# Which engine turns the softmax weights, pair by pair, and how turned blocks travel, in a two-layer attention kernel

## Chip, cores and metric

One core of a Trainium2 chip. The metric is the device time of one execution in microseconds.

## The reference

Sixteen batch entries of 256 tokens x 256 channels go through two layers. Layer 0 is attention of x on ctx_1024 with 16 heads of 64 channels, an output product, a residual and a layer norm. Layer 1 is masked self attention (16 heads of 16), cross attention on ctx_1024 (16 heads of 16), and an MLP of width 1024, each with residual and layer norm. Cut to what matters, one attention is

```python
scores = jnp.einsum('bqhd,bkhd->bhqk', qh, kh) / jnp.sqrt(jnp.float32(hd))
scores = jnp.where(mask != 0, jnp.finfo(scores.dtype).min, scores)
p = jax.nn.softmax(scores, axis=-1)
out = jnp.einsum('bhqk,bkhd->bqhd', p, vh)
```

All three attentions are over 256 keys. They are called A (layer 0), B (self) and C (cross).

## The kernel before

Scores are computed with queries on the partitions, so that the softmax sums run along the free dimension. The weighing of the values contracts over the keys, so every 256 x 256 matrix of softmax weights must be turned, keys onto the partitions.

**Pairs, quads, places.** Heads go two at a time as pairs (e = 0 and 1) and four at a time as quads; an attention has 8 pairs, 4 quads. The kernel is software pipelined over batch entries: a body works on five of them at once (streams x, a, b, c, m). Twelve bodies are full (n = 4 to 15); four fill the pipeline and a last one, written out by hand in `last_schedule`, empties it. A full body has 24 places, one for each pair, in the quad order AAABCBACBBCC: A0 to A5 are places 0 to 5, B0 B1 are 6 and 7, C0 C1 8 and 9, B2 B3 10 and 11, A6 A7 12 and 13, C2 C3 14 and 15, B4 to B7 16 to 19, C4 to C7 20 to 23.

**The list of steps.** `Line.advance` writes one list of steps, and each engine walks through it in this order and does the steps that are its own, with semaphores between the engines. An engine's queue is in order. A place g holds:
- S: TensorE computes the scores of the pair into two of three PSUM banks (ps_s0, ps_s1, ps_av in rotation); VectorE (`extremes`, L1071) masks them and takes the extreme of each row, in four instructions, into the prob tile. TensorE may begin the next place's S when the first head of this one is masked.
- R: VectorE takes the reciprocals of the previous place's pair (L1081), for which ScalarE's sums must be there; then POOL (`normalize`, L1182) scales this pair's two heads by them and counts up `normed`. POOL's residual steps (L1173, L1161, L1170) come after.
- D: VectorE's `turn_blocks` (L1093) turns 32 x 32 blocks of the pair two places back into the tile `blocks`; SyncE's `spill` (L595) writes it with four DMAs to DRAM. L: `load_back` (L602), a place later, reads it into `prob_b`, keys on the partitions.
- T0, T1: TensorE turns one head each of the pair three places back (L797) into ps_t0 and ps_t1. VectorE (L1102) copies a first pair of a quad out, ScalarE (L911) a second pair.
- jobs: the projections, output products and MLP parts set down for this place (`after` in `schedule`), with their evacuations on VectorE or ScalarE.
- W: TensorE weighs the values with the quad whose second pair is four places back (L820), in full bodies into ps_t1. X: ScalarE's exponentials of this place's pair (L901). AV: the weighed values are copied out, by ScalarE or, for every other quad of B and C, VectorE (L1114).

In full bodies the first pair of each quad, whichever attention, is turned by VectorE in blocks through DRAM, at even places only, and the second by TensorE, with tile `prob_t`. In the other bodies TensorE turns both. The order at a place is S, R, D, L, T0, jobs, W, T1, X, AV. SyncE's queue issues all transfers, in the order of the list.

Of the kernel before, what the change touches and what calls it, by code (L numbers as in the profile page):

```python
# [11 lines left out]
F32 = mybir.dt.float32  # L12
# [5 lines left out]
P = 128  # L18
# [22 lines left out]
BLOCKED = {(s, q) for s in "ABC" for q in range(QUADS)}  # L41
# [23 lines left out]
class Line:  # L65
# [4 lines left out]
    def __init__(self, steps, carried, blocked):  # L70
        self.steps = steps
        self.pairs = {g - len(carried): (p[1:], b) for g, (p, b) in enumerate(carried)}
        self.blocked = blocked
        self.places = 0

    def score(self, *pair):
        self.pairs[self.places] = pair, (pair[0], pair[1] // 2) in self.blocked
        self.steps.append(("S",) + pair)

    def advance(self, jobs):  # L80


        g, pairs, steps = self.places, self.pairs, self.steps

        def older(back, parity, by_blocks=None):
            pair, blocked = pairs.get(g - back, (None, None))
            return pair if pair and pair[1] % 2 == parity and by_blocks in (None, blocked) else None
# [11 lines left out]
        weigh = older(LAG + 1, 1)  # L99
        quad = weigh and (weigh[0], weigh[1] // 2, weigh[2])  # L100
        if quad:
            steps.append(("W",) + quad)
        if turn:
            steps.append(("T1",) + turn)
# [235 lines left out]
def program(nc, io):  # L340
    with ExitStack() as ctx:
# [27 lines left out]
        x_t, c_t = sb("x_t", [P, DT, TOK]), sb("c_t", [P, DT, TOK])  # L369
# [6 lines left out]
        prob_t = sb("prob_t", [P, 2, TT, TOK])  # L376


        blocks = sb("blocks", [P, 4, TT * 2 * TT * SLOT])
        prob_b = sb("prob_b", [P, 2, 4, TT * 2 * TT * SLOT])  # L380
# [8 lines left out]
        v_next = sb("v_next", [P, TT, D])  # L389
# [22 lines left out]
        x_cols_in, c_cols_in = sem("x_cols_in"), sem("c_cols_in")  # L412
# [18 lines left out]
        spilled = sem("spilled")  # L431
        landed = [sem("landed0"), sem("landed1")]
        p_kept = [nc.dram_tensor(f"p_kept{i}", (P, 4, TT * 2 * TT * SLOT), F32) for i in range(2)]
# [24 lines left out]
        x_cols, c_cols = (tok_view(io[n]) for n in ("x_cols", "ctx_cols"))  # L458
# [46 lines left out]
        def _(sp):  # L505
# [9 lines left out]
            def load_columns(body, step):  # L515
# [8 lines left out]
                sp.dma_start(c_t[:, :, :].unsqueeze(1), c_cols[:, bass.ds(b, 1)]).then_inc(c_cols_in, 16)  # L524

# [60 lines left out]
            def spill(body, step):  # L586

                _, s, p, _ = step
                n = body.turned_so(body.quad(step), True)
                sp.wait_ge(flipped, n + 1)  # L590
                if n >= 2:
                    sp.wait_ge(landed[n % 2], 16 * (n // 2))
                by_key = p_kept[n % 2].rearrange("(g r) q x -> q r g x", r=SLOT)
                for q in range(4):
                    sp.dma_start(by_key[q], blocks[q * SLOT:(q + 1) * SLOT, :, :]).then_inc(spilled, 16)  # L595

            def load_back(body, step):
                n = body.turned_so(body.quad(step), True)
                sp.wait_ge(spilled, 64 * (n + 1))
                (_, s0, p0, _), b0 = body.pair_at(body.place(step) - 4)  # L600
                sp.wait_ge(weighed[s0], count(b0, QUADS, p0 // 2 + 1))
                sp.dma_start(prob_b[:, body.quad(step) % 2], p_kept[n % 2][:, :, :]).then_inc(landed[n % 2], 16)  # L602
# [22 lines left out]
            for body in bodies():  # L625
                for step in body.steps:
                    if step[0] == "D":
                        spill(body, step)
                    elif step[0] == "L":
                        load_back(body, step)  # L630
# [13 lines left out]
        def _(pe):  # L644
# [49 lines left out]
            def job(body, step):  # L694
# [8 lines left out]
                if name in ("q", "k"):  # L703
# [3 lines left out]
                    last = columns_out(ps, wq0 if name == "q" else wk0, 2 * i, x_t if name == "q" else c_t)  # L707
# [5 lines left out]
                elif name == "kc":  # L713
                    if first:
                        pe.wait_ge(w_in["attn1"], 16)
                    last = columns_out(ps, w1["ck"], 0, c_t)
# [61 lines left out]
            def turn(body, step, e):  # L778
# [4 lines left out]
                quad = body.quad(step)  # L783
                if p % 2 and not body.by_blocks[quad]:
                    pe.wait_ge(copied_first, 2 * body.turned_so(quad, False) + e + 1)
                elif quad:
                    pe.wait_ge(copied_second, 2 * (quad - 1) + e + 1)
# [13 lines left out]
            def weigh(body, step):  # L801
# [4 lines left out]
                firsts = body.turned_so(n, by_blocks)  # L806
                if by_blocks:
                    pe.wait_ge(landed[firsts % 2], 16 * (firsts // 2 + 1))
                else:
                    pe.wait_ge(copied_first, 2 * (firsts + 1))  # L810
                pe.wait_ge(copied_second, 2 * (n + 1))
                by_query = prob_b[:, n % 2].rearrange("p q (k e t r) -> p k e t q r", k=TT, e=2, t=TT)
                by_head = prob_b[:, n % 2].rearrange("p q x -> p (q x)").rearrange("p (e k n) -> p e k n", e=2, k=TT)

                def weighted(out, w, j, e, kt, **tile):
                    by_block = j == 0 and by_blocks
                    turned_pair = by_query[:, kt, e] if by_block else (prob_t[:, e, kt] if j else by_head[:, e, kt])
                    if by_block:
                        out = out.rearrange("p (t q r) -> p t q r", t=TT, r=SLOT)
# [415 lines left out]
```

## Time and profile before

| what | value |
|---|---|
| median of 3 runs | 1815.4 us (1813.83 to 1820.91) |
| profiled execution, its time | 1820.59 us |
| its span, first to last instruction | 1818.4 us |
| TensorE matmul busy | 1714.5 us (94%), 11328 instructions |
| VectorE busy | 1270.7 us (70%), 4778 |
| ScalarE busy | 1190.7 us (65%), 3985 |
| POOL busy | 985.4 us (54%), 1014 |
| mean granted TensorE clock | 0.988 |
| SyncE's DMA queue | 321.73 MB, 56.3% of the 16 engines' span |

Times are microseconds from the first instruction unless marked ns. Busy means that an instruction is under way; a matmul's end is modelled and matmuls overlap, so what one costs is read from start to start. In a list of groups, "idle" is the time in which the engine stood still just before them, behind the arrow what ended it.

### The profile page before, as it was taken

How to read it: one execution, taken by the hardware profiler on the slowest of the kernel's cores; microseconds unless marked ns; L12 is line 12 of the kernel's file. 1: busy time of each engine (PE TensorE's matmuls, PEld its weight loads, DVE VectorE, ACT ScalarE, POOL GpSimd, SP SyncE). 2: the span in 40 equal slices, each digit the busy share in tenths (PEclk: the TensorE clock that was granted, in tenths of full speed). 3: DMA queues.
4: the chain of work that ended last, by engine and by line, in shares of the span. 5: the costliest groups of instructions: out<-in, count | busy, mean ns of one | idle time of the engine just before them, and what ended most of it. 6: DMA issues, size and time to landing. Idle time of an engine off the chain costs nothing.

```text
span 1818.4 us, 36921 instructions
## 1 busy us (share of the span) xinstructions
PE 1714.5 (94%) x11328; PEld 1284.8 (71%) x11328; DVE 1270.7 (70%) x4778; ACT 1190.7 (65%) x3985; POOL 985.4 (54%) x1014
## 2 busy tenths in 40 slices
PE   8999999999999999999999999999999999998887
PEld 6777677777777777677777767777777777776556
DVE  4465766786768778676877858687786867667763
ACT  4374866667676666767666666776667677566752
POOL 2252745547465564747556464655647465455742
PEclk9999999999999999999999999999999999998899
DMA  7222226685766768576676847668575766613010
GB/s 252 89 97 100 82 79 216 181 279 158 238 192 203 251 172 277 163 249 185 204 250 175 280 134 240 207 192 264 179 253 158 242 214 175 198 65 134 30 58 12
DMA packets 215696, 324.11 MB, mean 178 GB/s; under 512 B 22992, under 2 KB 184144, under 8 KB 207056
## 3 DMA queue, kind: packets, MB, share of 16 engines
q1 hardware_dynamic: 215360, 321.73, 56.3%
q8 instruction: 95, 1.56, 0.4%
q14 instruction: 97, 0.79, 0.1%
q10 hardware_dynamic: 144, 0.03, 0.0%
HBM read 170.68 MB, written 150.99 MB: 177 GB/s over the span
## 4 chain that ended last, share of the span: by engine, by line
PE 77%; DMA 7%; DVE 6%; ACT 5%; SPq 3%; issue 2%; POOL 0%; POOLq 0%; DVEq 0%; ACTq 0%
PE ps_g L654 45%; PE ps_t L797 10%; PE ps_s L773 8%; PE ps_t L820 8%; DMA prob_b<-p_kept 4%; ACT prob L901 3%; DMA p_kept<-blocks 3%; PE ps_av L773 3%; PE ps_av L820 3%; DVE prob L1071 2%; SPq L595 1%; SPq L578 1%; PE ps_g L660 1%; DVE prob_b L1102 1%; DVE blocks L1093 1%
## 5 line engine op out<-in xcount | busy, mean ns | idle before, releaser
L1182 POOL TENSOR_TENSOR prob<-prob,recip 128x512 f32<-128x512 f32 x768 | 788.2, 1048 | 668.4 <-DVE recip L1081 668.1
L901 ACT ACTIVATE prob<-prob,ext 128x256 f32<-128x256 f32 x1536 | 757.2, 499 | 11.9 <-DVE ext L1071 11.5
L911 ACT ACTIVATE prob_t<-ps_t 128x512 f32<-128x512 f32 x384 | 226.4, 594 | 397.2 <-PE ps_t L797 396.5
L797 PE MATMUL ps_t<-ident,prob 128*128 128x128 f32 x1920 | 304.1, 283 | 7.2 <-DVE prob_b L1102 5.4
L901 ACT ACTIVATION_READ_ACCUMULATOR prob<-prob,ext 128x1 f32 x1536 | 295.6, 192 | 0.0
L797 PEld LDWEIGHTS ps_t<-ident,prob 128*128 128x128 f32 x1920 | 216.7, 142 | 93.3 <-issue 49.7
L1071 DVE CUSTOM_DVE_ANT_0 prob<-ps_s,mask_a 128x256 f32<-128x256 f32 x392 | 145.4, 421 | 84.0 <-PE ps_s L773 70.6
L1093 DVE STREAM_TRANSPOSE blocks<-prob 128x512 f32<-128x512 f32 x288 | 183.9, 676 | 3.1 <-POOL prob L1182 2.2
L1071 DVE CUSTOM_DVE_ANT_0 prob<-ps_s,zero 128x256 f32<-128x256 f32 x392 | 144.4, 418 | 47.0 <-PE ps_av L773 39.6
L1071 DVE CUSTOM_DVE_ANT_0 prob<-ps_s,mask_b 128x256 f32<-128x256 f32 x368 | 136.0, 417 | 24.3 <-PE ps_s L773 14.7
L773 PE MATMUL ps_s<-k_ctx,q 64*128 64x256 f32 x784 | 144.8, 402 | 5.5 <-DVE ext L1071 3.1
L654 PE MATMUL ps_g<-wo,k_ctx 128*128 128x256 f32 x512 | 121.0, 392 | 22.6 <-ACT k_ctx L920 21.6
L654 PE MATMUL ps_g<-x_t,wq 128*128 128x256 f32 x512 | 124.3, 386 | 5.8 <-DMA wq<-L_xattn_Wq 5.8
L1071 DVE DVE_READ_ACCUMULATOR2_ANT ext<- 128x1 f32 x1536 | 126.7, 82 | 0.0
L654 PEld LDWEIGHTS ps_g<-wo,k_ctx 128*128 128x128 f32 x512 | 97.2, 194 | 40.5 <-issue 26.1
L654 PE MATMUL ps_g<-c_t,wk 128*128 128x256 f32 x512 | 125.6, 388 | 0.0
L654 PE MATMUL ps_g<-x_t,wl 128*128 128x256 f32 x512 | 123.1, 384 | 1.2 <-ACT x_t L880 1.2
L654 PE MATMUL ps_g<-wv,c_t 128*128 128x256 f32 x512 | 121.0, 379 | 0.0
L654 PE MATMUL ps_g<-wl,h_t 128*128 128x256 f32 x512 | 116.8, 383 | 2.0 <-issue 2.0
L773 PEld LDWEIGHTS ps_s<-k_ctx,q 64*128 64x128 f32 x784 | 87.5, 186 | 32.6 <-issue 28.9
L654 PEld LDWEIGHTS ps_g<-x_t,wq 128*128 128x128 f32 x512 | 94.9, 192 | 19.4 <-issue 6.4
L654 PEld LDWEIGHTS ps_g<-wl,h_t 128*128 128x128 f32 x512 | 96.2, 192 | 14.9 <-issue 2.7
(104 smaller groups left out, 2967.7 us busy)
## 6 DMA issues: line engine op xcount, KB each, us to landing
p_kept<-blocks SPq DMA_DIRECT2D x576, 128.0 KB, 2.5
prob_b<-p_kept SPq DMA_DIRECT2D x144, 512.0 KB, 3.4
k_parts_C<-k_hl SPq DMA_DIRECT2D x64, 256.0 KB, 3.1
k_parts_B<-k_hl SPq DMA_DIRECT2D x64, 256.0 KB, 3.0
q_parts_B<-q_hl SPq DMA_DIRECT2D x64, 256.0 KB, 3.4
k_B<-k_parts_B SPq DMA_DIRECT2D x16, 1024.0 KB, 7.4
q_B<-q_parts_B SPq DMA_DIRECT2D x16, 1024.0 KB, 7.2
q_parts_C<-k_hl SPq DMA_DIRECT2D x64, 256.0 KB, 4.9
```

Of the source, the lines that this page charges most:

```text
L578: sp.dma_start(q_parts[s][:, part].rearrange("e r c t -> (r c) e t"), parts[:, part // 2]).then_inc(q_saved[s], 16)
L595: sp.dma_start(by_key[q], blocks[q * SLOT:(q + 1) * SLOT, :, :]).then_inc(spilled, 16)
L654: last = nc.tensor.matmul(out, lhs[i], rhs[i], start=i == 0, stop=i == n - 1)
L660: last = nc.tensor.transpose(ps[:, d, t * P:(t + 1) * P], src[:, t, d * P:(d + 1) * P], ident[:, :])
L773: last = nc.tensor.matmul(two(score_bank(body, step, e))[:, t, :], q[r, t * P:(t + 1) * P], k[r], start=True, stop=True)
L797: last = nc.tensor.transpose(two(ps_t[e])[:, kt, qt * P:(qt + 1) * P], src[:, e, qt, kt * P:(kt + 1) * P], ident[:, :])
L820: return nc.tensor.matmul(out, w, turned_pair, start=kt == 0, stop=kt == TT - 1, **tile)
L901: last = nc.scalar.activation(tile, tile, ACT.Exp, bias=ext[:, slot, e, t:t + 1], scale=-1.0, accum_out=sums[:, slot, e, t:t + 1])
L911: nc.scalar.activation(prob_t[:, e], two(ps_t[e]), ACT.Copy).then_inc(copied_second, 1)
L1071: last = nc.vector.tensor_tensor_reduce(out=prob[:, slot, e, t, :], in0=two(score_bank(body, step, e))[:, t, :], in1=mask, scale=-SCALE[s] ...
L1093: last = nc.vector.transpose(out[:, kt], src[:, kt])
L1182: nc.gpsimd.tensor_tensor(rows, rows, recip[:, slot, e].unsqueeze(2) .to_broadcast([P, TT, TOK]), ALU.mult).then_inc(normed[s], 1)
```

## The change

Which pairs are turned how. In full bodies all pairs of A and C (16 of 24) are now turned by VectorE in blocks, all pairs of B (8) by TensorE. The first pair of a B quad is copied out of PSUM by VectorE, the second by ScalarE; both now land in `prob_b`, and `prob_t` is gone.

How the blocks travel. `blocks` and `prob_b` hold both pairs of a quad and are double. `turn_blocks` is one instruction over 1024 columns instead of two over 512. DRAM is not used any more: after the second pair of a quad is turned, SyncE's `exchange` issues four DMAs of 256 KB straight from the partitions of `blocks` to those of `prob_b`, when the quad two before has been weighed. That needs another order of the keys: a new input `ctx_keys` holds the context in that order, and the masks of A are permuted likewise; a tile `c_k` takes its columns for the key projections. It shares its memory with `v_next`, so that its load waits for `v_saved`.

Order in a place. D stands first, in front of S (`begin` is called by `score`). Where TensorE turns a first pair at a place that also has a W, T1 follows T0 directly, ahead of jobs and W, and W waits for VectorE's copies of both. The order is D, S, R, T0, (T1), jobs, W, (T1), X, AV.

```diff
-BLOCKED = {(s, q) for s in "ABC" for q in range(QUADS)}
+BLOCKED_BATCHES = {"A": range(3, 15), "C": range(1, 13)}
+BLOCKED = {(s, q) for s in "AC" for q in range(QUADS)}
...
+    def begin(self):
+
+        if self.begun == self.places:
+            self.begun += 1
+            if self.older(BLOCKS, None, True):
+                self.steps.append(("D",) + self.older(BLOCKS, None, True))
 
     def score(self, *pair):
+        self.begin()
         self.pairs[self.places] = pair, (pair[0], pair[1] // 2) in self.blocked
         self.steps.append(("S",) + pair)
 
     def advance(self, jobs):
...
+        self.begin()
         if g - 1 in pairs:
             steps.append(("R",) + pairs[g - 1][0])
-        if older(BLOCKS, 0, True):
-            steps.append(("D",) + older(BLOCKS, 0, True))
-        if older(BLOCKS + 1, 0, True):
-            steps.append(("L",) + older(BLOCKS + 1, 0, True))
-        turn = older(LAG, 0, False) or older(LAG, 1)
+        turn = older(LAG, None, False)
+        weigh = older(LAG + 1, 1)
+        quad = weigh and (weigh[0], weigh[1] // 2, weigh[2])
+        early = turn and turn[1] % 2 == 0 and quad and self.blocked
         if turn:
             steps.append(("T0",) + turn)
+        if early:
+            steps.append(("T1",) + turn)
         steps.extend(jobs)
...
         if quad:
             steps.append(("W",) + quad)
-        if turn:
+        if turn and not early:
             steps.append(("T1",) + turn)
...
@@ load_columns
                 sp.dma_start(c_t[:, :, :].unsqueeze(1), c_cols[:, bass.ds(b, 1)]).then_inc(c_cols_in, 16)
+                sp.wait_ge(v_saved, count(b - 1, 16, 16))
+                sp.dma_start(c_k[:, :, :].unsqueeze(1), c_keys[:, bass.ds(b, 1)]).then_inc(c_keys_in, 16)
...
@@ spill and load_back, now exchange
+            def exchange(body, step):
+
+                quad = body.quad(step)
+                n = body.turned_so(quad, True)
+                sp.wait_ge(flipped, 2 * n + 2)
+                (_, s0, p0, _), b0 = body.pair_at(2 * quad - 4)
+                sp.wait_ge(weighed[s0], count(b0, QUADS, p0 // 2 + 1))
                 for q in range(4):
...
+                    sp.dma_start(prob_b[:, quad % 2, q].rearrange("p j x -> p (j x)"),
+                                 blocks[q * SLOT:(q + 1) * SLOT, n % 2].rearrange("r g j x -> r g (j x)")
+                                 ).then_inc(landed[n % 2], 16)
...
             sp.dma_start(c_t[:, :, :], c_cols[:, 0]).then_inc(c_cols_in, 16)
+            sp.dma_start(c_k[:, :, :], c_keys[:, 0]).then_inc(c_keys_in, 16)
...
@@ weigh
+                if by_blocks:
+                    k = body.turned_so(n, True)
+                    pe.wait_ge(landed[k % 2], 64 * (k // 2 + 1))
+                pe.wait_ge(copied_second, 2 * body.turned_so(n + 1, False))
+                if body.full:
+                    pe.wait_ge(copied_first, 2 * body.turned_so(n + 2, False))
...
@@ turn_blocks
+                n = body.turned_so(body.quad(step), True)
                 dve.wait_ge(normed[s], count(body.batch(step), HEADS, 2 * p + 2))
...
-                for kt in range(TT):
-                    last = nc.vector.transpose(out[:, kt], src[:, kt])
-                last.then_inc(flipped, 1)
+                if n >= 2 and p % 2 == 0:
+                    dve.wait_ge(landed[n % 2], 64 * (n // 2))
+                src = prob[:, body.slot(step, P_RING)].rearrange("p e t (k g r) -> p (e t k) g r", k=TT, r=SLOT)
+                out = blocks[:, n % 2, :, p % 2].rearrange("p g (m q) -> p m g q", q=SLOT)
+                nc.vector.transpose(out, src).then_inc(flipped, 1)
```

## Rows read from the trace of the kernel before

**Rows 1.** Page, the chain that ended last: shares of the span.
```profile
PE 77%; DMA 7%; DVE 6%; ACT 5%; SPq 3%; issue 2%; POOL 0%; POOLq 0%; DVEq 0%; ACTq 0%
```

**Rows 2.** Waits: engine line <- what it waited for: us, times, longest.
```profile
DVE prob L1071 <- PE ps_s L773: 178.5, 144, 4.5
...
DVE prob L1071 <- PE ps_av L773: 62.4, 48, 6.2
...
PE ps_s L773 <- DVE ext L1071: 20.0, 23, 2.3
...
DVE blocks L1093 <- POOL prob L1182: 2.2, 12, 0.2
```

**Rows 3.** Windows: us, busy (x instructions) by engine, clock, DMA share, GB/s.
```profile
445.00:1500.00 1055.00, 1018.87 (x6769) 764.18 (x6771) 781.99 (x2945) 731.90 (x2459) 609.06 (x622) 1.00 0.69 214
...
1660.00:1680.00 20.00, 14.65 (x105) 10.07 (x105) 16.17 (x60) 14.42 (x49) 9.98 (x11) 0.83 0.45 158
```

**Rows 4.** Timeline of SyncE: start, us; two issues one body apart.
```profile
902.46 0.38 SPq L571 DMA_DIRECT2D k_C<-k_parts_C  x1
...
1008.37 0.38 SPq L571 DMA_DIRECT2D k_C<-k_parts_C  x1
```

**Rows 5.** Timeline, PE at place 0: half a turn, then a projection.
```profile
902.46 0.66 PE L797 MATMUL ps_t<-ident,prob 128*128 128x128 f32 x4
...
902.95 1.89 PE L654 MATMUL ps_g<-w_l,ctx_B 128*128 128x256 f32 x8
```

**Rows 6.** Timeline, DVE at places 0 and 1: start, duration.
```profile
902.69 0.42 DVE L1071 CUSTOM_DVE_ANT_0 prob<-ps_s,mask_a 128x256 f32<-128x256 f32 x1 [0.79 <-PE ps_s L773]
...
904.17 1.27 DVE L1093 STREAM_TRANSPOSE blocks<-prob 128x512 f32<-128x512 f32 x2
...
905.37 0.65 DVE L1029 TENSOR_TENSOR res_ln<-ps_g,res_ln 128x512 f32<-128x512 f32 x1
...
908.56 0.41 DVE L1071 CUSTOM_DVE_ANT_0 prob<-ps_av,mask_a 128x256 f32<-128x256 f32 x1
...
912.62 0.68 DVE L986 COPY v<-ps_g 128x512 f32<-128x512 f32 x1
```

**Rows 7.** Groups by form, VectorE's copies: xcount | busy, mean ns | idle.
```profile
L1102 DVE COPY prob_b<-ps_t 128x512 f32<-128x512 f32 x96 | 64.4, 675 | 44.7 <-PE ps_t L797 44.2
```

**Rows 8.** Timeline: DVE and POOL where a turn waits for POOL.
```profile
966.84 0.18 DVE L1081 RECIPROCAL recip<-sums 128x4 f32<-128x4 f32 x1
...
967.10 3.04 POOL L1182 TENSOR_TENSOR prob<-prob,recip 128x512 f32<-128x512 f32 x3 [0.89 <-DVE recip L1081]
...
969.17 1.30 DVE L1093 STREAM_TRANSPOSE blocks<-prob 128x512 f32<-128x512 f32 x2 [0.18 <-POOL prob L1182]
```

**Rows 9.** Timeline, DVE: first extremes of places 7, 11, 14, 17, 21.
```profile
937.63 0.42 DVE L1071 CUSTOM_DVE_ANT_0 prob<-ps_av,mask_b 128x256 f32<-128x256 f32 x1 [0.28 <-PE ps_s L773]
...
955.17 0.39 DVE L1071 CUSTOM_DVE_ANT_0 prob<-ps_s,mask_b 128x256 f32<-128x256 f32 x1
...
966.96 0.42 DVE L1071 CUSTOM_DVE_ANT_0 prob<-ps_s,zero 128x256 f32<-128x256 f32 x1
...
980.17 0.42 DVE L1071 CUSTOM_DVE_ANT_0 prob<-ps_s,mask_b 128x256 f32<-128x256 f32 x1 [0.84 <-PE ps_av L773]
...
998.09 0.39 DVE L1071 CUSTOM_DVE_ANT_0 prob<-ps_s,zero 128x256 f32<-128x256 f32 x1
```

**Rows 10.** Timeline, DVE at place 21: reciprocal.
```profile
1000.37 0.18 DVE L1081 RECIPROCAL recip<-sums 128x4 f32<-128x4 f32 x1 [0.85 <-ACT prob L901]
```

**Rows 11.** Timeline, POOL at place 7: first residual step.
```profile
941.93 1.28 POOL L1173 TENSOR_TENSOR res_ln<-res_ln,rows 128x512 f32<-128x512 f32 x1
```

**Rows 12.** Timeline, PE at place 18: output product.
```profile
985.06 1.10 PE L654 MATMUL ps_g<-wo,k_ctx 128*128 128x256 f32 x4 [1.72 <-ACT k_ctx L920]
```

**Rows 13.** DMA issues: xcount, KB each, median us to landing.
```profile
p_kept<-blocks SPq DMA_DIRECT2D x576, 128.0 KB, 2.5
...
q_B<-q_parts_B SPq DMA_DIRECT2D x16, 1024.0 KB, 7.2
```

More of the change, by code:

```diff
@@ L73, in __init__, with older @@
         self.blocked = blocked
-        self.places = 0
+        self.places = self.begun = 0
+    def older(self, back, parity=None, by_blocks=None):
+        pair, blocked = self.pairs.get(self.places - back, (None, None))
+        return pair if pair and parity in (None, pair[1] % 2) and by_blocks in (None, blocked) else None
+    def begin(self):
[3 more added lines that the diff above has]
+                self.steps.append(("D",) + self.older(BLOCKS, None, True))
     def score(self, *pair):
+        self.begin()
         self.pairs[self.places] = pair, (pair[0], pair[1] // 2) in self.blocked
@@ L457, in program @@
         x_d, m_d, o_d = (tok_view(io[n]) for n in ("x", "mask_BxSxS2_bf0", "out"))
-        x_cols, c_cols = (tok_view(io[n]) for n in ("x_cols", "ctx_cols"))
+        x_cols, c_cols, c_keys = (tok_view(io[n]) for n in ("x_cols", "ctx_cols", "ctx_keys"))
         wide = lambda n: io[n].rearrange("(k p) n -> p k n", p=P)
@@ L626, in _ @@
                 for step in body.steps:
[L627 to L630, printed above, removed]
+                    if step[0] == "D" and step[2] % 2:
+                        exchange(body, step)
                     elif step[0] == "IO":
@@ L715, in job @@
                         pe.wait_ge(w_in["attn1"], 16)
-                    last = columns_out(ps, w1["ck"], 0, c_t)
+                    pe.wait_ge(c_keys_in, count(b, 16, 16))
+                    last = columns_out(ps, w1["ck"], 0, c_k if b in BLOCKED_BATCHES["C"] else c_t)
                 elif name == "vc":
@@ L781, in turn @@
                 pe.wait_ge(normed[s], count(body.batch(step), HEADS, 2 * p + e + 1))
[L783 to L787, printed above, removed]
+                n = body.turned_so(body.quad(step), False)
+                if p % 2:
+                    pe.wait_ge(copied_first, 2 * n + e + 1)
+                elif n:
+                    pe.wait_ge(copied_second, 2 * (n - 1) + e + 1)
                 if e == 1:
@@ L909, in evac_turned @@
                 quad = body.quad(step)
-                act.wait_ge(turned, 2 * (quad + body.turned_so(quad + 1, False)) + e + 1)
-                nc.scalar.activation(prob_t[:, e], two(ps_t[e]), ACT.Copy).then_inc(copied_second, 1)
+                act.wait_ge(turned, 2 * (2 * body.turned_so(quad, False) + 1) + e + 1)
+                out = prob_b[:, quad % 2].rearrange("p q j x -> p (q j x)")[:, (2 + e) * 512:(3 + e) * 512]
+                nc.scalar.activation(out, ps_t[e][:, :], ACT.Copy).then_inc(copied_second, 1)
             def evac_weighed(body, step):
@@ L1100, in evac_turned @@
                 quad = body.quad(step)
-                dve.wait_ge(turned, 2 * (quad + body.turned_so(quad, False)) + e + 1)
-                nc.vector.tensor_copy(prob_b[:, quad % 2].rearrange("p q x -> p (q x)")[:, e * 512:(e + 1) * 512],
-                                      ps_t[e][:, :]).then_inc(copied_first, 1)
+                dve.wait_ge(turned, 2 * 2 * body.turned_so(quad, False) + e + 1)
+                out = prob_b[:, quad % 2].rearrange("p q j x -> p (q j x)")[:, e * 512:(e + 1) * 512]
+                nc.vector.tensor_copy(out, ps_t[e][:, :]).then_inc(copied_first, 1)
             def evac_weighed(body, step):
@@ L1215, in laid_out @@
     arrays["x_cols"] = np.swapaxes(given["x"], 1, 2)
+    by_block = lambda a: np.swapaxes(a.reshape(*a.shape[:-1], TT, SLOT, P // SLOT), -1, -2).reshape(a.shape)
+    arrays["ctx_keys"] = by_block(np.swapaxes(given["ctx_1024"], 1, 2))
+    mask = given["mask_BxSxS2_bf0"].copy()
+    for b in BLOCKED_BATCHES["A"]:
+        mask[b] = by_block(mask[b])
+    arrays["mask_BxSxS2_bf0"] = mask
     arrays["ctx_cols"] = np.swapaxes(given["ctx_1024"], 1, 2)
```

64 lines of the change are left out of this document (19 added, 45 removed).

## The prediction

> **What bounds the kernel now.** I read the chain of waits first: TensorE holds 77% of it, DMA 7%, VectorE 6% [rows 1]. Then the list of waits: VectorE waits for a score product 178.5 and 62.4 us in all (two banks), TensorE for VectorE's extremes 20.0 us, and a turn of VectorE's for POOL 2.2 us [rows 2]. So TensorE sets the pace, VectorE runs just behind it with short rests. Third, the windows: from 445 to 1500 us TensorE is busy 1018.87 of 1055, 97%, VectorE 74%, at a granted clock of 1.00 [rows 3]. One full body takes 1008.37 - 902.46 = 105.9 us, between two issues of the same DMA [rows 4]; it has 24 places, 4.4 us each, and there are 12 full bodies. I number places 0 (A0) to 23 (C7) and write S7 for the start of VectorE's extremes of place 7.
>
> **What the change takes from TensorE.** Before, TensorE turns 12 pairs of a body, after only B's 8. Half a pair holds the engine from 902.46 to 902.95, 0.49 us [rows 5], a pair about 1.0. Four pairs are 4 us of a body, 48 us in all (2.7%), if TensorE remains the limit. ScalarE loses 16 copies of a body; it lies beside TensorE and I count nothing. The weighing keeps its number of products.
>
> **What it gives VectorE.** Before: 12 turns at 1.20 us (904.17 to 905.37 [rows 6]), 14.4. After: 16 at the same price (one instruction of 1024 columns for two of 512), 19.2; bounds for one turn are the two instructions' 1.27 on top and 1.1 below, if a start is saved. Each B quad's first pair also needs two copies from PSUM of 675 ns [rows 7], eight in a body, 5.4. VectorE gets 10 us more: 74% of 105.9 is 78.5, so 88.7 of a body. As a mean that still fits.
>
> **Where it does not fit: the order of the turn.** Before, VectorE took at a place: the extremes, the reciprocal of the previous pair, then the turn of the pair two back, then jobs. The turn came after the extremes, and at even places only. Now the turn stands in front of the extremes, at 16 of 24 places. It waits until POOL has scaled both heads of the pair two back, and POOL starts that when VectorE has done the pair's reciprocal, which stands behind the previous place's extremes. Behind the waiting turn stand this place's extremes, on which ScalarE's exponentials and TensorE's next scores depend. This closes a ring over four steps:
> extremes to the next instruction after the reciprocal 904.17 - 902.69 = 1.48 [rows 6], of which the reciprocal's step is 0.09; reciprocal to the end of POOL's scaling, seen where a turn does wait for POOL: 966.84 to 969.17, 2.33 [rows 8]; turn 1.20. So 1.39 + 2.33 + 1.20 = 4.92 us from S to S wherever a turn stands in front, however short TensorE's work there is. Jobs of the place run inside the 2.33; where they are longer, they replace it.
>
> Hence one body, in five stretches, after against before (the starts in [rows 9], the body's end 105.91 later):
> - S21 to S7, ten intervals, each with a turn in front: 10 x 4.92 = 49.2. Jobs of place 0 run 905.37 to 908.56, 3.19, and those of place 1 from 910.04 (S1 at 908.56 plus 1.48) to some 913.24, 3.2 [rows 6]; each makes 1.48 + 3.2 + 1.2 = 5.9, so 1.0 more, twice. The reciprocal of place 20's pair waited 0.85 for ScalarE [rows 10] and still will. 52.0. Before 1043.54 - 998.09 = 45.5.
> - S7 to S11: POOL is late first. From S7: 1.65 to its start, then scaling 2.04, the two residual steps of place 7 at 1.28 and a gap, 2.6 [rows 8, 11], two more scalings, turn 1.24: 11.6 to S10; then 4.9. 16.5. Before 17.5.
> - S11 to S14: 1.65, three scalings 6.1, three residual steps 3.9 (1.3 each), turn 1.24: 12.9. Before 11.8.
> - S14 to S17: three rings, 14.8. Before 13.2.
> - S17 to S21: one turn fewer in front, and TensorE's work is as before (one pair less at 18, one more at 19): 17.9 before, with a wait of 1.72 of the output product for ScalarE [rows 12] that is shorter by perhaps 0.4. 17.5.
>
> Sum 113.7, before 105.9: 7.8 a body, 93 us in twelve. Inside it lies one more new wait: at place 13 the weighing of C0 has no job ahead of it and must wait for VectorE's two copies, as ps_t1 holds both; TensorE's scores and turn end 2.1 us after place 13's start, the copies 1.3 + 1.5 + 1.3 = 4.1 after it, 2 us. There VectorE, not TensorE, sets the next S, so it is not added. The TensorE saving is hidden by the ring wherever S is late.
>
> **DMA.** Spill and load go (12 x 1 MB moved in a body), 8 exchanges of 1 MB come, each from the second pair's turn on, four issues. Nearest rows: four spills are 128 KB each, 2.5 us to landing; the 1 MB load of spread queries 7.2 us [rows 13]. With 1.8 us of issue the exchange takes between 4.3 and 9.0 us. Time to have it hidden: shortest at place 17 (A3): turn done at S15, S15 to S17 is 9.8; TensorE may start place 17 when half the extremes of 16 are done, 0.8 after S16, so 4.1 before S17, and the weighing follows 0.4 behind the scores: 6.1 us. At others over 7. I take 6 us, nothing; at 9.0, 2.9 at place 17 and up to 2 more at places 5 and 3, of which half reaches S: 3 us a body, 35 us. The Trainium skill (DMA: Bandwidth & Descriptors, Anatomy of one DMA) fits a DMA from the other issue path with 2.0 us plus bytes over 436 GB/s; by that 1 MB is an estimated 4.4 us, nothing would be late, and the sum stays 113.7. No run so far shows an exchange between partitions. The new loads of ctx_keys wait for the saved values at place 17, one DMA; exchanges behind it come at place 23. At the start 256 KB stand ahead of the weights: 1 us.
>
> **Sum.** The profiled execution took 1820.6 us (span 1818.4), the median of the runs is 1815.4. 1820.6 + 93 + 1 = 1914.6; less the same 5.2 that the profiled one stands above the median: 1909.
>
> **Rivals.**
> 1. *TensorE stays the limit.* VectorE waits for TensorE anyway, 178.5 us in all, and the ring runs in that shadow. For it: the turn in front uses just this rest. Against: the rest is (178.5 + 62.4) / 16 = 15 us a batch, 0.6 a place, while TensorE's places of the first stretch would shrink to (45.5 - 4 pairs + 1) / 10, 4.3 us, against a ring of 4.92. It decides if the ring is under some 4.3 us, POOL's part under 1.7. Then -48, +24 for place 13 (2 us x 12): 1791.
> 2. *The gain and the ring cancel.* If VectorE catches up at the places with much TensorE work better than I count, half of each stretch's excess is lost: at most 0.5% from before, 1815.
> 3. *The exchange is late, the ring is not the bound.* At 9 us it misses by 2.5 at place 17, 1.4 at 7 and about 1.5 at 3, where it stands behind the query saves on SP's queue: 5.4 a body, 65 on top of rival 1: 1856.
> 4. *The clock falls too.* TensorE's work of a body, 102.3 less 4, is 86% of 113.7. At 1660 to 1680, where it was busy 73%, the granted clock was 0.83, part of the time the lower of the two levels, 1.2 GHz [rows 3]. On the ring TensorE's speed costs nothing; on the last stretch, S7 to S9 and place 11, some 30 us a body, a clock of 0.9 costs up to 3: 36 us more, 1945. For it that row; against it that no wait in the ring is over 2.5 us.
>
> **How the numbers follow.** The ring alone 0.62; with a fallen clock or late exchange 0.22; rival 3 alone 0.03; rival 2 0.04; rival 1 0.09. A measurement here tells about 0.5% from no change. Slower: 0.87, same 0.04, faster 0.09. The predicted time is 1909. The range reaches down to 1850, where the ring costs 3 us a body instead of 7.8 (turns at 1.1, and TensorE ahead more often), and up to 1955 for a fallen clock; this leaves out rivals 1 and 2 and little above.
>
> **What would show it.** The body is 113 to 114 us; VectorE's blocks<-prob waits for POOL's scaling at most of 16 places, some 170 us in all, up to 2.2 us each at places without jobs, where before it waited 2.2 us in all; TensorE's scores wait for the extremes, far over 20 us; TensorE's share in the windows falls from 97% to about 90%, its turns are 1536 products in place of 1920. S to S is 4.9 from place 2 to place 7. The forecast is wrong if the turns are found waiting for nothing, with TensorE still at 96%; if the scores hold the turn's place open; or if the weighing waits for prob_b<-blocks in place of VectorE.

## The result: slower by 11.7%, and what the profile shows

The changed kernel takes 2032.1 us, the median of four runs (2012.0 to 2041.1), against 1815.5 of the kernel before: ratio 1.117 [1.108, 1.126]. Forecast were 1909 and a range up to 1955, so the sign was right and the size was 123 us short. The profiled execution took 2041.1 us, with a span of 2039.3. The rows of this section are read from it.

From the page: busy times, shares of the chain that ended last, the DMA groups of the exchange and of the spread queries (KB each, median us to landing).
```profile
PE 1778.2 (87%) x10944; PEld 1295.8 (64%) x10944; DVE 1385.0 (68%) x4778; ACT 1113.6 (55%) x3793; POOL 984.8 (48%) x1014
...
PE 55%; DVE 15%; issue 8%; SPq 7%; DMA 7%; POOL 4%; ACT 3%; DVEq 0%; POOLq 0%
...
prob_b<-blocks SPq DMA_DIRECT2D x384, 256.0 KB, 4.8
q_B<-q_parts_B SPq DMA_DIRECT2D x16, 1024.0 KB, 9.3
```
TensorE held 77% of the chain before [rows 1] and holds 55% now. VectorE, POOL, SyncE's queue and the engine's own issue have taken the rest. TensorE is busy 87% of the span, no other engine more than 68%, so most of the loss must lie in waits of one engine for another; a second part, TensorE's lower clock, comes up in the windows.

The list of waits: us in all, times, longest.
```profile
ACT prob L907 <- DVE ext L1078: 289.0, 158, 4.4
DVE prob L1078 <- PE ps_s L778: 168.4, 120, 6.5
...
PEld ps_t L826 <- DMA prob_b<-blocks: 117.8, 40, 6.1
PE ps_t L826 <- DMA prob_b<-blocks: 104.2, 39, 5.7
...
DVE blocks L1099 <- POOL prob L1187: 100.9, 96, 2.2
...
DVE prob L1078 <- PE ps_av L778: 68.1, 13, 8.3
...
PE ps_s L778 <- DVE ext L1078: 33.1, 43, 2.4
```
Two waits are new. VectorE's turn waits for POOL's scaling 100.9 us, against 2.2 [rows 2], and never over 2.2 us at once. The weighing waits for the exchange 104.2 us, up to 5.7 us at once; no such wait stands in [rows 2]. The prediction named this second wait as a sign that it is wrong. (The `PEld` row is the weight load for the same products, not a second cost.)

The windows of the steady part, the columns of [rows 3].
```profile
445.00:1500.00 1055.00, 913.69 (x5558) 659.77 (x5558) 749.69 (x2527) 576.58 (x1988) 525.69 (x538) 0.93 0.53 148
```
TensorE is busy 87% of it (before 97%), at a granted clock of 0.93 (before 1.00).

SyncE's timeline, the issue that gave the body's length in [rows 4], first and last of eleven bodies.
```profile
390.69 0.55 SPq L576 DMA_DIRECT2D k_C<-k_parts_C  x1
...
1759.36 0.55 SPq L576 DMA_DIRECT2D k_C<-k_parts_C  x1
```
1368.67 / 11 = 124.4 us a body. Before it was 106.6 by the same mean (105.9 in the body that the prediction used); forecast 113.7. The 17.8 us a body, twelve times, are 214 of the 217 us lost.

VectorE's timeline of one body, the first extremes of places 7, 11, 14, 17 and 21, which answer to [rows 9].
```profile
1056.42 0.39 DVE L1078 CUSTOM_DVE_ANT_0 prob<-ps_av,mask_b 128x256 f32<-128x256 f32 x1
...
1075.96 0.39 DVE L1078 CUSTOM_DVE_ANT_0 prob<-ps_s,mask_b 128x256 f32<-128x256 f32 x1
...
1088.66 0.39 DVE L1078 CUSTOM_DVE_ANT_0 prob<-ps_s,zero 128x256 f32<-128x256 f32 x1
...
1104.26 0.39 DVE L1078 CUSTOM_DVE_ANT_0 prob<-ps_s,mask_b 128x256 f32<-128x256 f32 x1
...
1123.04 0.42 DVE L1078 CUSTOM_DVE_ANT_0 prob<-ps_s,zero 128x256 f32<-128x256 f32 x1 [1.07 <-PE ps_s L778]
```
With the same starts of the experiments below, one body of each, this gives the five stretches of the prediction (the first ends at S7 and begins at S21 of the body before):

| us | S21 to S7 | S7 to S11 | S11 to S14 | S14 to S17 | S17 to S21 | sum |
|---|---|---|---|---|---|---|
| before (prediction's body) | 45.5 | 17.5 | 11.8 | 13.2 | 17.9 | 105.9 |
| forecast | 52.0 | 16.5 | 12.9 | 14.8 | 17.5 | 113.7 |
| after | 56.1 | 19.5 | 12.7 | 15.6 | 18.8 | 122.7 |
| no exchange | 54.2 | 16.3 | 12.7 | 17.1 | 18.8 | 119.0 |
| turn after extremes | 51.0 | 21.5 | 14.1 | 13.3 | 23.0 | 122.9 |
| neither | 49.4 | 15.9 | 14.1 | 15.0 | 17.2 | 111.7 |
| neither, copies by ScalarE | 47.0 | 15.9 | 12.9 | 13.3 | 17.2 | 106.4 |

A single body can stand off the mean: over the full bodies "neither" has a mean of 110.0 us, the others 119.5 (no exchange), 122.3 (turn after extremes) and 107.2 (the last row).

### The profile page after: what moved, and what is told of

It is laid out like the page before. It is cut to its first block, busy times and chain, and to the rows that moved or that the text cites. A ratio compares the mean times of both kernels' runs of the same rounds, so it can differ in the third digit from the quotient of the medians.

```text
span 2039.3 us, 35276 instructions
## 1 busy us (share of the span) xinstructions
PE 1778.2 (87%) x10944; PEld 1295.8 (64%) x10944; DVE 1385.0 (68%) x4778; ACT 1113.6 (55%) x3793; POOL 984.8 (48%) x1014
## 4 chain that ended last, share of the span: by engine, by line
PE 55%; DVE 15%; issue 8%; SPq 7%; DMA 7%; POOL 4%; ACT 3%; DVEq 0%; POOLq 0%
PE ps_g L652 32%; PE ps_t L802 7%; PE ps_t L826 6%; DVE prob L1078 6%; PE ps_s L778 5%; SPq L599 5%; DMA prob_b<-blocks 4%; POOL prob L1187 4%; PE ps_av L826 2%; DMA q_parts_C<-k_hl 2%; SPq L583 2%; DVE res_ln L1054 2%; ACT prob L907 1%; DVE blocks L1099 1%; PE ps_av L778 1%
## 5 line engine op out<-in xcount | busy, mean ns | idle before, releaser
L1099 DVE STREAM_TRANSPOSE blocks<-prob 128x1024 f32<-128x1024 f32 x192 | 237.8, 1238 | 102.1 <-POOL prob L1187 100.9
L802 PE MATMUL ps_t<-ident,prob 128*128 128x128 f32 x1536 | 241.8, 287 | 6.2 <-DVE prob_b L1108 5.1
L918 ACT ACTIVATE prob_b<-ps_t 128x512 f32<-128x512 f32 x192 | 112.7, 596 | 218.5 <-PE ps_t L802 217.9
L826 PE MATMUL ps_t<-prob_b,v 128*64 128x256 f32 x768 | 134.1, 510 | 101.5 <-DMA prob_b<-blocks 101.5
L802 PEld LDWEIGHTS ps_t<-ident,prob 128*128 128x128 f32 x1536 | 172.0, 144 | 71.6 <-issue 36.9
L826 PEld LDWEIGHTS ps_t<-prob_b,v 128*64 128x64 f32 x768 | 67.0, 180 | 155.6 <-DMA prob_b<-blocks 113.5
L1108 DVE COPY prob_b<-ps_t 128x512 f32<-128x512 f32 x192 | 124.6, 672 | 45.7 <-PE ps_t L802 45.2
L652 PE MATMUL ps_g<-wo,k_ctx 128*128 128x256 f32 x512 | 133.3, 421 | 24.2 <-ACT k_ctx L927 23.2
L652 PE MATMUL ps_g<-x_t,wq 128*128 128x256 f32 x512 | 137.4, 417 | 7.0 <-DMA wq<-L_xattn_Wq 7.0
L894 ACT ACTIVATE k_ctx<-ps_g,columns 128x256 f32<-128x256 f32 x128 | 53.2, 466 | 119.6 <-PE ps_g L652 119.5
```

What stands on the lines that cost most here:

```text
L652: last = nc.tensor.matmul(out, lhs[i], rhs[i], start=i == 0, stop=i == n - 1)
L802: last = nc.tensor.transpose(two(ps_t[e])[:, kt, qt * P:(qt + 1) * P], src[:, e, qt, kt * P:(kt + 1) * P], ident[:, :])
L826: return nc.tensor.matmul(out, w, turned_pair, start=kt == 0, stop=kt == TT - 1, **tile)
L894: last = nc.scalar.activation(out[:, c, :], ps[:, m, :], ACT.Relu if name == "h" else ACT.Identity, bias=bias[:, c:c + 1])
L918: nc.scalar.activation(out, ps_t[e][:, :], ACT.Copy).then_inc(copied_second, 1)
L1099: nc.vector.transpose(out, src).then_inc(flipped, 1)
```

## The experiments

Theory 1: the ring of the prediction, closed by the turn's place in front of the extremes, costs most. Theory 2: the exchange arrives late. The first three runs take the two apart.

**No exchange.** The weighing reads the turned tile itself. `prob_b` plays no part for A and C, and VectorE's turn waits, in place of the landing, until the quad that held its buffer has been weighed. What this kernel leaves out is the crossing of the partitions.

```diff
-                    if step[0] == "D" and step[2] % 2:
-                        exchange(body, step)
...
-                    pe.wait_ge(landed[k % 2], 64 * (k // 2 + 1))
+                    pe.wait_ge(flipped, 2 * k + 2)
...
-                by_query = [prob_b[:, n % 2, :, j]
+                by_query = [blocks[:, k % 2, :, j]
```

> The weighing reads the blocks where VectorE left them, without any exchange (so the weighed values of A and C are left wrong in full bodies); the turn still stands in front. Theory ring (VectorE turn waits for POOL, about 4.9 us from extremes to extremes, is a bound of its own): a body of about 114 us, 1910 to 1930 us in all, the turns still waiting some 100 to 170 us for POOL. Theory exchange (the late transfer is the whole loss and the ring lies in its shadow): about 1800 us.

Measured: 1970.1 us, 1.082 [1.079, 1.085]. Waits:
```profile
DVE blocks L1100 <- POOL prob L1188: 129.7, 108, 2.2
```
Without any exchange some 150 us of loss remain (the kernel before took 1819.1 us in this round).

**The turn after the extremes.** The exchange stays; D goes back behind R.

```diff
 begin:
-            if self.older(BLOCKS, None, True):
-                self.steps.append(("D",) + self.older(BLOCKS, None, True))
 advance, behind R:
+        if older(BLOCKS, None, True):
+            steps.append(("D",) + older(BLOCKS, None, True))
```

> The changed kernel with the turn put back behind extremes and reciprocal of its place. Theory ring: the 7.8 us a body of the prediction go, 93 us, to about 1940 us, and the turns wait under 10 us for POOL. Theory exchange: the exchange starts 1.4 us later at each quad and the weighings wait that much longer, 2030 us or more.

Measured: 2013.6 us, 1.106 [1.102, 1.109]. Waits:
```profile
PE ps_t L826 <- DMA prob_b<-blocks: 143.8, 47, 5.1
```
No wait of a turn for POOL is in its list, so the ring is open, and yet only 18.5 us come back, hardly more than the spread of the runs (the two intervals touch): the wait for the exchange grew from 104 to 144 us.

**Neither**, both edits at once.

> Both: no exchange (weighed values wrong in full bodies) and the turn behind the extremes. Theory that these two are all of the loss: what is left is TensorE less four pairs a body plus the wait at place 13, 1790 to 1815 us. If a third cause exists (VectorE's 10 us more of work a body), 1830 or more.

Measured: 1857.8 us, 1.021 [1.018, 1.025]. That is 174 us under the changed kernel, where the two edits alone gave 62 and 18.5. The ring alone costs 1970.1 - 1857.8 = 112 us, the exchange alone 2013.6 - 1857.8 = 156, both together 174, not 268. The two costs overlap. If they are two bounds on the same starts, at each place only the later one counts; a run below tests that. And 1857.8 is above the 1830 that the expectation gave for a third cause.

**SyncE's queue in another order.** The save of the self queries, the load of the cross values and the load of the cross queries are issued later, behind exchanges.

```diff
-        ("A", 0): late + [dma("save k", "B"), job("ks"), dma("save q", "B")],
-        ("A", 1): [dma("k", "B"), job("qs"), ln("ln1"), job("v", 0)],
-        ("A", 2): [job("x2T"), dma("q", "B"), job("q", 2), job("qc"), io("value_c")],
+        ("A", 0): late + [dma("save k", "B"), job("ks")],
+        ("A", 1): [dma("k", "B"), job("qs"), dma("save q", "B"), ln("ln1"), job("v", 0)],
+        ("A", 2): [job("x2T"), dma("q", "B"), job("q", 2), job("qc")],
...
-        ("A", 4): [dma("q", "C"), job("oc"), job("vs")],
-        ("A", 5): [ln("ln2")],
+        ("A", 4): [job("oc"), job("vs")],
+        ("A", 5): [dma("q", "C"), io("value_c"), ln("ln2")],
```

> The changed kernel with four steps moved in SyncE's queue so that no exchange of places 1, 3 and 5 stands behind a save of queries or the load of values or of C's queries. Theory that the place in the queue makes the exchange late: the exchanges of A0 and A1 start 3.4 and 5.7 us earlier, and 5 to 7 us a body go, to 1950 to 1975 us. Theory that issue and transfer are the delay: within 1% of the changed kernel, 2015 to 2050 us.

Measured: 2024.1 us, 1.112 [1.109, 1.116], as the second theory had it and not the first. But the place in the queue does matter at each single place: place 7 became short (2.58 us instead of 5.51), place 5 as much longer (9.80 instead of 6.80). The longest wait moved from one exchange to another and the sum stayed.

**The kernel before with its turns in front.** The twelve turns of [rows 6] are put ahead of the extremes; all else is the kernel before.

```diff
     def score(self, *pair):
+        pair2, blocked2 = self.pairs.get(self.places - BLOCKS, (None, None))
+        if pair2 and pair2[1] % 2 == 0 and blocked2:
+            self.steps.append(("D",) + pair2)
...
-        if older(BLOCKS, 0, True):
-            steps.append(("D",) + older(BLOCKS, 0, True))
```

> The kernel before with one change: its turns, still at even places only, stand in front of the extremes. Theory ring, needed only where it is longer than the place: intervals into even places that are under 4.85 us fall short by 9 us a body, but every second interval has no turn in front and gives most of it back: 1 to 3 us a body, 1830 to 1855 us. If the position of the turn alone were the price, whatever the spacing, half of e1's ring cost of 9.4 us a body: 1870 us.

Measured: 1829.5 us, 1.009 [1.006, 1.012]. Waits:
```profile
DVE blocks L1094 <- POOL prob L1183: 108.3, 76, 2.2
```
The turn waits 108 us for POOL, as much as in the changed kernel, and it costs 15 us. With a turn only at even places the place between catches up. The wait in a list is not the price. The same wait stands in a kernel that loses 112 us by it; what differs is that there turns stand at neighbouring places, and that the granted clock is 0.95 there and 0.99 here.

**Neither, and ScalarE copies the first pairs of B.** This takes the new wait of place 13 away.

```diff
 evac_turned (ScalarE):
+                if step[2] % 2 == 0:
+                    if body.full:
+                        act.wait_ge(turned, 2 * 2 * body.turned_so(quad, False) + e + 1)
+                        out = prob_b[:, quad % 2].rearrange("p q j x -> p (q j x)")[:, e * 512:(e + 1) * 512]
+                        nc.scalar.activation(out, ps_t[e][:, :], ACT.Copy).then_inc(copied_first, 1)
+                    return
 the copy on VectorE:
-                if step[2] % 2:
+                if step[2] % 2 or body.full:
                     return
```

> e3 (no exchange, turn behind the extremes; weighed values wrong in full bodies) with the first pairs of B copied out of PSUM by ScalarE in full bodies. Theory third cause (the weighing of C0 and B2 at places 13 and 21 waits for VectorE's copies, which stand behind extremes and reciprocal): places 13 and 21 fall by 2 and 1 us, 30 to 45 us in all, to 1815 to 1830 us. If the rest is VectorE's load, 5.4 of its 10 us more are gone and the gain is spread over many places, to about the same time; if it is neither, 1850 to 1860 us.

Measured: 1825.4 us, 1.007 [1.005, 1.009]. From 1.021 this is some 27 us, 32 by the bare times (the kernel before took 1819.1 us in one round and 1814.3 in the other). In the bodies of the table place 13 falls from 4.59 to 3.42 us and place 21 from 5.44 to 5.01, 1.6 us in all or 19 us in twelve bodies. Place 14 falls as well, from 7.37 to 5.69, and place 6 from 4.91 to 3.23, though neither holds a wait for a copy. In "neither" the granted clock was 0.78 at place 14 and 0.65 at place 6; here it is 1.00 at all 24 places.

**Exchange pair by pair.** On top of "turn after extremes" each pair leaves as soon as it is turned, eight DMAs of 128 KB a quad instead of four of 256 KB.

```diff
-                    if step[0] == "D" and step[2] % 2:
+                    if step[0] == "D":
...
-                sp.wait_ge(flipped, 2 * n + 2)
+                sp.wait_ge(flipped, 2 * n + j + 1)
...
-                    sp.dma_start(prob_b[:, quad % 2, q].rearrange("p j x -> p (j x)"),
-                                 blocks[q * SLOT:(q + 1) * SLOT, n % 2].rearrange("r g j x -> r g (j x)")
+                    sp.dma_start(prob_b[:, quad % 2, q, j],
+                                 blocks[q * SLOT:(q + 1) * SLOT, n % 2, :, j]
```

> e2 with each pair exchanged on its own as soon as it is turned (eight issues of 128 KB a quad instead of four of 256 KB). Theory that bytes in flight behind the second turn make the exchange late: half of the megabyte is gone by then, the waits for it fall from about 13 us to 4 us a body, 1900 to 1930 us. Theory that each issue costs about 1 us whatever its size: eight issues keep the queue as late as four, 2010 us or more.

Measured: 1905.1 us, 1.051 [1.046, 1.055]. The page's DMA group and the waits:
```profile
prob_b<-blocks SPq DMA_DIRECT2D x768, 128.0 KB, 2.9
...
PE ps_t L827 <- DMA prob_b<-blocks: 59.1, 25, 4.8
```
108 us come back, of the 156 that the exchange alone costs. That fits the first theory, that it matters how much is still to be moved when the second turn ends. It was not separated from the shorter issues: one of 128 KB holds the queue for a median of 0.60 us, one of 256 KB for 1.02.

**Pair by pair, further.** Three kernels on top of the last one: with ScalarE's copies; with these and the queue order above; and with the load of the spread self queries moved from place 2 to place 3 as well.

```diff
-        ("A", 2): [job("x2T"), dma("q", "B"), job("q", 2), job("qc")],
-        ("A", 3): [job("k", 2), dma("save q", "C"), job("v", 1)],
+        ("A", 2): [job("x2T"), job("q", 2), job("qc")],
+        ("A", 3): [dma("q", "B"), job("k", 2), dma("save q", "C"), job("v", 1)],
```

> e8 without the moved steps in SyncE's queue. Theory that e8's queue order hurts at place 5 (the load of spread queries waits there in front of the exchange) as much as it helps at place 3 and 7: 1865 to 1885 us. If the queue was worth its 3 to 4 us a body: 1905 us less ScalarE's part, some 1900 us or more.

Measured: 1877.0 us, 1.034 [1.029, 1.039].

> e7 with ScalarE's copies of e6 and the steps of e4 in SyncE's queue. If each of the three takes its own wait: 1860 to 1890 us. If the exchange stays the bound: as e7.

Measured: 1872.8 us, 1.034 [1.030, 1.038], no different from the one without the queue order.

> e8 with the load of B's queries moved one place on, behind the exchange of A0's second pair. Theory head of the line: place 5 falls from 8.2 us to the 4.1 of e6, 4 us a body, 1825 to 1840 us. If the transfer itself is late there: within 1% of 1873 us. A time under that of the kernel before would need the exchange free, and e6 says that even then it is 0.7% slower.

Measured: 1854.3 us, 1.021 [1.016, 1.027], above the 1825 to 1840 expected. Place 5 fell from 8.19 to 4.06 us, as expected; place 7 is now 7.6, which was not. The groups, weighing of A; then SyncE and TensorE at place 7:
```profile
L827 PE MATMUL ps_t<-prob_b,v 128*64 128x256 f32 x768 | 93.5, 385 | 22.8 <-DVE v L998 15.0 <-DMA prob_b<-blocks 7.8
...
958.88 0.59 SPq L588 DMA_DIRECT2D q_C<-q_parts_C  x1
...
966.80 0.35 PE L779 MATMUL ps_s<-k_C,q_C 64*128 64x256 f32 x1 [3.43 <-issue]
```
The exchange is hidden (7.8 us left) and a product takes 385 ns. Place 7 is long for another reason: the first scores of C need the load of the cross queries, which the new order of the queue has put behind the exchanges. It is issued at 958.88 and lands at 966.72, and TensorE, after 3.43 us of standing still, begins at 966.80. The late transfer moved once more, from an exchange to this load. This is the fastest complete version with the changed split of the pairs, and it is still about 2% slower than before.

**Pair by pair with the turn in front.** If the two costs are two bounds and not a sum, the early exchange must bring the changed kernel down to "no exchange" and no further.

> The changed kernel, turn in front, with each pair exchanged on its own. Theory of two bounds, of which the longer sets the time: the exchange falls under the ring, which e1 showed at 119.4 us a body; 1975 to 1995 us. If the two delays simply add up, e7's gain of 108 us comes here too: 1925 us.

Measured: 1977.6 us, 1.090 [1.084, 1.095], with a body of 119.3 us; "no exchange" has 119.0. The early exchange gives 54 us back here, and 108 with the turn behind the extremes, so a sum is excluded and the time stops where "no exchange" stands, as two bounds would have it.

**Through DRAM again**, pair by pair, turn after the extremes: four DMAs spill each pair, one of 1 MB loads the quad.

> e7 with each pair spilled to DRAM by the four DMAs and one load of 1 MB after the second, as the kernel before did it for one pair of a quad. Theory that the direct path is what the change gains: the load adds about 5 us behind the second pair's spill, most weighings of A and C wait for it, 2000 us or more. If the hop is hidden: as e7, 1905 us.

Measured: 2215.3 us, 1.220 [1.215, 1.226]. Waits:
```profile
PE ps_t L834 <- DMA prob_b<-p_kept: 338.5, 68, 9.1
```
The load can start only when the second pair's spill has landed, and SyncE's queue, with all that stands in it, waits for that. Two transfers one after the other are later than one direct exchange, so the direct way as such is not the fault.

## Why the prediction was wrong: its ring held, 123 us were missing

The direction and the ring held; the sum failed at two terms that it put at nothing. It gave the clock nothing ("On the ring TensorE's speed costs nothing"): without any exchange the time is 1970 us, 61 over the forecast, and most of that excess stands where the granted clock was low. And it gave the exchange nothing ("I take 6 us, nothing"): that is worth the other 62.

**Right: the ring.** VectorE and POOL of the changed kernel at place 10 (start, duration).
```profile
1072.46 0.17 DVE L1088 RECIPROCAL recip<-sums 128x4 f32<-128x4 f32 x1
...
1074.79 1.25 DVE L1099 STREAM_TRANSPOSE blocks<-prob 128x1024 f32<-128x1024 f32 x1 [2.15 <-POOL prob L1187]
...
1075.96 0.39 DVE L1078 CUSTOM_DVE_ANT_0 prob<-ps_s,mask_b 128x256 f32<-128x256 f32 x1
...
1072.72 2.04 POOL L1187 TENSOR_TENSOR prob<-prob,recip 128x512 f32<-128x512 f32 x2 [1.92 <-DVE recip L1088]
```
Reciprocal at 1072.46, POOL's two heads 1072.72 to 1074.76, turn at 1074.79, extremes at 1075.96. From the reciprocal to the turn 2.33 us, forecast 2.33; the turn 1.17, forecast 1.20. S10 stood at 1071.08, so 4.88 from S to S, forecast 4.92. Without exchange it is 4.84 or 4.85 at places 3, 6, 10, 15 and 16. The turns' wait for POOL came to 101 us (130 without exchange) where I forecast some 170; it stood at 96 turns, since at the other places jobs or the exchange are later than POOL.

**Wrong step 1: "On the ring TensorE's speed costs nothing."** The prediction held that jobs of a place run inside the 2.33 us, priced them for places 0 and 1 alone, and left a fallen clock to rival 4, outside the sum, with "no wait in the ring is over 2.5 us" against it. VectorE of the changed kernel at place 2.
```profile
1029.10 0.17 DVE L1088 RECIPROCAL recip<-sums 128x4 f32<-128x4 f32 x1
1030.15 0.69 DVE L990 TENSOR_TENSOR q<-ps_g,columns 128x512 f32<-128x512 f32 x1 [0.89 <-PE ps_g L652]
1032.02 0.69 DVE L1021 TENSOR_TENSOR k_hl<-ps_g,columns 128x512 fp32r<-128x512 f32 x1 [1.18 <-PE ps_g L652]
...
1033.54 1.24 DVE L1099 STREAM_TRANSPOSE blocks<-prob 128x1024 f32<-128x1024 f32 x1
1034.69 0.38 DVE L1078 CUSTOM_DVE_ANT_0 prob<-ps_s,mask_a 128x256 f32<-128x256 f32 x1
```
0.89 and 1.18 us of waiting for TensorE stand in front of the turn: POOL is not the releaser, and the place takes 6.94 where 4.92 was forecast. Place 14 of the kernel without exchange is of the same kind, 7.38 from S to S.
```profile
1051.25 0.69 DVE L1035 TENSOR_TENSOR res_ln<-ps_g,res_ln 128x512 f32<-128x512 f32 x1 [2.98 <-PE ps_g L650]
```
Why the products come late stands in the windows of places 2, 14 and 18 (columns of [rows 3]), three of the kernel without exchange, then three of the one that has neither and lets ScalarE copy.
```profile
990.96:997.91 6.95, 6.95 (x30) 5.40 (x29) 4.85 (x16) 2.23 (x9) 2.04 (x2) 0.81 0.90 320
1046.75:1054.13 7.38, 7.38 (x39) 5.90 (x41) 4.27 (x16) 3.04 (x10) 2.94 (x4) 0.90 0.01 2
1068.78:1073.49 4.71, 4.71 (x18) 3.51 (x17) 1.54 (x10) 2.08 (x8) 2.04 (x2) 0.65 0.70 222
...
922.31:927.58 5.27, 5.27 (x30) 4.15 (x29) 4.73 (x15) 2.98 (x10) 2.04 (x2) 1.00 1.00 328
973.95:979.64 5.69, 5.69 (x33) 4.82 (x32) 4.30 (x16) 2.40 (x8) 2.29 (x3) 1.00 0.16 45
992.80:995.43 2.63, 2.63 (x16) 1.98 (x15) 1.55 (x11) 1.82 (x7) 1.00 (x1) 1.00 0.60 169
```
TensorE is busy all through in all six. Place 2 has 30 products in both kernels and takes 6.95 us at a granted clock of 0.81, 5.27 at 1.00. Place 14 takes 7.38 at 0.90 and 5.69 at 1.00, place 18 takes 4.71 at 0.65 and 2.63 at 1.00 (there a few products lie on the other side of the border). The same sixteen products of place 18, in the same two kernels:
```profile
1067.54 5.38 PE L650 MATMUL ps_g<-wo,k_ctx 128*128 128x256 f32 x16 [2.08 <-ACT k_ctx L926]
...
991.16 3.69 PE L650 MATMUL ps_g<-wo,k_ctx 128*128 128x256 f32 x16 [1.15 <-ACT k_ctx L930]
```
Before the clock fell, TensorE had stood still at place 1 for 2.23 us, for the layer norm that VectorE makes late:
```profile
989.42 0.63 PE L656 MATMUL ps_g<-ident,res_ln 128*128 128x128 f32 x4 [2.23 <-DVE res_ln L1053]
```
at place 13 for 2.06 us, for VectorE's copies; and at places 16 and 17 for 0.97 and 2.08 us. None is over 2.5 us, and no exchange takes part. So rival 4 came true beside the ring. The length of one wait does not decide it: with the turn after the extremes TensorE also stands still for 2.06 us at place 13, and the clock stays at 1.00.

By this comparison the lower clock costs 1.7, 1.7 and 2.1 us at the three places, 5.5 a body. That is an estimate; no run changes the clock alone. Even at full clock TensorE's work at places 2 and 14 (5.27 and 5.69) is longer than the ring's 4.92, 1.1 more; other places are a little under the forecast. Together 119.0 - 113.7 = 5.3 us a body, and 1970 - 1909 = 61 us in time. Rival 4 had up to 3 us a body, at other places.

**Wrong step 2: "I take 6 us, nothing" for the exchange.** SyncE's queue at places 2 to 5.
```profile
1037.80 0.32 SPq L556 DMA_DIRECT2D v_C<-v_kept  x1
1038.22 4.86 SPq L599 DMA_DIRECT2D prob_b<-blocks  x4
1043.12 3.81 SPq L583 DMA_DIRECT2D q_parts_C<-k_hl  x4
1050.09 0.33 SPq L588 DMA_DIRECT2D q_C<-q_parts_C  x1
1050.52 10.18 SPq L599 DMA_DIRECT2D prob_b<-blocks  x8
```
And TensorE's timeline at place 5.
```profile
1047.38 1.12 PE L826 MATMUL ps_t<-prob_b,v 128*64 128x256 f32 x4 [3.90 <-DMA prob_b<-blocks]
```
The second turn of the first A quad ends at 1033.54 + 1.24 = 1034.78. The exchange is first issued at 1038.22: 3.4 us behind the load of the cross values, which waits for that tile to come free. The four issues take 4.86 us, not 1.8: about 1.2 us each here. The weighing may begin at 1047.38, 4.3 us after the last issue. That makes 12.6 us from turn to use, of which 9.2 run from the first issue. The forecast's bounds were 4.3, from four spills of 128 KB, and 9.0, from one load of 1 MB [rows 13]; it took 6, and the measured one lies at the upper bound, with 4.86 us of issues where 1.8 were put. The 3.4 us in the queue stand in neither bound: a moved step stands behind every wait of the queue it moves to. The next exchange, for the weighing at place 7, is later still. Its second turn ends at 1044.8; it is issued at 1050.52, behind the load of the cross queries, which waits for their save to land, and TensorE begins at 1059.41, 14.6 us after the turn. Place 7 takes 5.51 us in this body, 1.50 without exchange. The Trainium skill (DMA: Bandwidth & Descriptors, Anatomy of one DMA), whose fit is for a DMA from another issue path, gave an estimated 4.4 us for the megabyte; here one 256 KB part alone needs a median of 4.8 us to landing. The measurement decides. In time: 2032 - 1970 = 62 us.

**A second price of the same wait.** Windows of the changed kernel: the 3.90 us of TensorE's wait, the 3.6 us after it, and the weighing at place 7.
```profile
1043.50:1047.40 3.90, 0.02 (x2) 0.02 (x2) 3.90 (x13) 1.87 (x7) 1.69 (x2) 0.99 0.97 283
1047.40:1051.00 3.60, 3.60 (x18) 1.79 (x18) 1.46 (x2) 0.20 (x2) 1.11 (x2) 0.54 0.41 142
1059.40:1061.30 1.90, 1.89 (x18) 1.08 (x18) 0.00 (x0) 0.00 (x0) 1.90 (x2) 1.00 0.95 204
```
After TensorE has stood still for 3.9 us the granted clock is 0.54, about the lower of the two levels, and the 18 products take 3.6 us. Those of place 7 come after a wait of 3.3 us, the clock stays at 1.00, and they take 1.9. So the long wait costs 1.7 us more than it lasts. The groups show it in the mean: weighing products of A take 510 ns here, and 385 where the exchange is hidden. So both causes, the ring's waits above and the exchange's here, bring rival 4's clock with them.

**The other steps.** The 1536 turn products are there, TensorE is busy 87% in the windows (forecast about 90, but part of the 87 is work at the lower clock), and the weighing at place 13 waits 2.06 us (forecast 2), from PE's timeline:
```profile
1086.11 1.07 PE L826 MATMUL ps_t<-prob_b,v_C 128*32 128x256 f32 x16 [2.06 <-issue]
```
It starts where VectorE's copies end; that these set it is shown by the run in which ScalarE makes them. TensorE's 4 us a body never came back as time. With ring, exchange and VectorE's copies all removed, the time is 1825, not the 1767 that 48 us less would make. In its body some places are shorter than before, 8.0 us in all; 4.4 of these lie at places 2, 7, 12 and 18 (5.27, 4.16, 4.72 and 2.63 us against 5.98, 5.72, 5.54 and 3.90). Others are longer, 7.9 us in all. Of these 5.2 lie at places 9, 13, 19 and 21 (6.54, 3.42, 6.48 and 5.01 against 5.72, 1.55, 5.66 and 3.31): these are the places at which TensorE now turns a first pair of B, and at 13 and 21 it also waits 0.90 and 0.56 us for the copies. Another 2.3 lie at places 5 and 15 (4.05 and 4.48 against 2.87 and 3.35); what makes those two longer was not tried.

**Left open.** Why the issue of a 256 KB exchange takes about 1.0 us and that of a 128 KB one 0.6. Bytes alone are not it: in the changed kernel the four saves of the self queries, 256 KB each, were issued in 1.99 us. And which part of each loss is the clock's was estimated from the traces, never set apart by a run.

## What to carry to other kernels

Before an instruction is moved ahead of the one that feeds the others, follow the loop it closes through every engine and count its place in each period: in the kernel before, a turn in front at every second place cost 15 us; in the changed one, with sixteen of 24, it cost 112. Ask also what TensorE's added waits do to its clock at the next places where it is the limit. A step moved to a queue is paid from the moment its input is ready: what it stands behind, its issues, and its landing, and the largest of such times must be compared with the shortest room. Two late things on the same chain need not add, so mending one of them alone shows little; judge a mend only with the other one gone.

## What the runs showed of the hardware

- Four copies of 256 KB from SBUF to SBUF across partitions, issued by SyncE: in the exchange shown they held its queue for 4.86 us and the last one landed 4.3 us later, 9.2 us for 1 MB; another was issued in 4.24 us. Eight of 128 KB, begun at the first turn, save 108 us a run.
- The route through DRAM with the same trigger, where the queue also waits for the spills, costs 2215 us against 1905.
- Waits of TensorE of 2.2 and 3.9 us were followed by a granted clock of 0.81 and 0.54, one of 3.3 us and one of 2.06 us by 1.00. At the lower clock sixteen products took 5.38 us, at 1.00 they took 3.69.
- The block turn of 128x1024 takes 1.17 us from start to start, about as long as the two of 128x512 did (1.20). POOL's scaling of two heads took 2.04 us before and after.
